# Gates in SBUF of their own between the marks of the next batch's front, and the back-transposes in the bank of the value products

## The reference

```python
q, k = x @ Wq, x @ Wk                                  # 16 heads of 64
w, sel = top_k(x @ Ws, 2)                              # per token and head, 2 of 8 experts
mix_v = sum_k sigmoid(w) * one_hot(sel)                # "gates"
v = einsum('bthe,bted->bhtd', mix_v, x @ Wv)           # "values"
probs = softmax(q * scale @ k^T)                       # 512 x 512 a head
attn = einsum('bhij,bhjd->bihd', probs, v)             # "heads"
mask_o = one_hot(top_k(x @ Wd, 2)).sum()               # also of "gates"
res = einsum('bthe,bthd,efd->bthf', mask_o, attn, Wo)  # "mixed" and "result"
```

## Time and profile before

| | |
|---|---|
| median of 3 runs | 3077.64 us (3067.38 to 3088.6) |
| the profiled execution, its own time | 3074.05 us |
| its span | 3072.2 us, 45343 instructions |
| PE busy | 2509.0 us (82%) |
| DVE busy | 1559.2 us (51%) |
| ACT busy | 1348.7 us (44%) |
| POOL busy | 808.0 us (26%) |
| mean granted TensorE clock | 0.919 |

### The profile page before, as it was taken

How to read it: one execution, slowest core, us unless ns; L and a number is a source line. 1 busy time by engine, 2 the same in 40 slices (tenths; PEclk the granted TensorE clock), 3 DMA queues, 4 the chain that set the end, 5 groups by cost and what they waited for, 6 DMA issues and landing times. The chain is left out here.

```text
span 3072.2 us, 45343 instructions
## 1 busy us (share of the span) xinstructions
PE 2509.0 (82%) x15660; PEld 1542.5 (50%) x15660; DVE 1559.2 (51%) x2646; ACT 1348.7 (44%) x2913; POOL 808.0 (26%) x370
## 2 busy tenths in 40 slices
PE   3984699779897898879897798978988798986476
PEld 2353346554475445654465544744456544653254
DVE  4235753546635384464735465353844557337622
ACT  0231226553464525554264534545255543653254
POOL 1003520106401092013701064011910136004500
PEclk7896799999898998999899998989999999999798
DMA  2110010112001030012101030011200121001001
GB/s 74 41 48 8 11 52 1 39 31 74 15 15 42 24 77 2 15 56 49 40 1 54 17 76 12 15 42 42 60 2 15 56 55 32 15 15 39 0 29 32
DMA packets 210737, 101.65 MB, mean 33 GB/s; under 512 B 137367, under 2 KB 189620, under 8 KB 210492
## 3 DMA queue, kind: packets, MB, share of 16 engines
q1 hardware_dynamic: 205052, 95.74, 11.3%
q10 hardware_dynamic: 5440, 2.75, 0.3%
HBM read 77.48 MB, written 20.99 MB: 32 GB/s over the span
## 5 line engine op out<-in xcount | busy, mean ns | idle before, releaser
L1508 DVE TENSOR_REDUCE nmax<-bank 128x1 f32<-128x512 f32 x512 | 340.9, 686 | 654.4 <-PE bank L971 652.5
L689 POOL TENSOR_TENSOR prod<-pv,mixv 128x1024 f32<-128x1024 f32 x184 | 608.5, 3343 | 239.9 <-ACT pv L1133 168.1
L1169 ACT ACTIVATE prT<-bank 128x512 f32<-128x512 f32 x512 | 305.5, 597 | 666.8 <-PE bank L704 662.3
L971 PE MATMUL bank<-keys,qs 64*128 64x512 f32 x1024 | 325.7, 714 | 245.2 <-DVE on L1502 99.8
L628 POOL TENSOR_TENSOR rstd<-vareps,minus_half 128x4 f32<-128x4 f32 x48 | 50.0, 1042 | 1474.9 <-DVE vareps L1276 1474.8
L1182 ACT ACTIVATE pr<-bank,nmax 128x512 f32<-128x512 f32 x512 | 349.4, 685 | 97.6 <-DVE nmax L1508 97.1
L704 PEld LDWEIGHTS bank<-ident,pr 128*128 128x128 f32 x2048 | 244.9, 152 | 267.1 <-issue 234.5
L704 PE MATMUL bank<-ident,pr 128*128 128x128 f32 x2048 | 357.8, 301 | 25.9 <-ACT prT L1169 25.8
L1075 ACT ACTIVATE arena<-bank 128x512 f32<-128x512 f32 x256 | 152.8, 597 | 467.0 <-PE bank L816 422.9
L1008 PE MATMUL bank<-prT,vals 128*64 128x128 f32 x4096 | 297.1, 290 | 59.1 <-ACT prT L1169 58.8
L1473 DVE TENSOR_REDUCE vals<-prod 128x128 f32<-128x1024 f32 x256 | 306.5, 1207 | 36.7 <-POOL prod L689 36.7
(11 more groups left out here) (220 smaller groups left out, 3064.7 us busy)
## 6 DMA issues: line engine op xcount, KB each, us to landing
Wg<-in_L_ffn_Wg SPq DMA_DIRECT2D x64, 256.0 KB, 2.8
Wu<-in_L_ffn_Wu SPq DMA_DIRECT2D x64, 256.0 KB, 3.1
Wd<-in_L_ffn_Wd SPq DMA_DIRECT2D x64, 256.0 KB, 3.8
out_rows<-on SPq DMA_DIRECT2D x32, 512.0 KB, 2.6
onR<-out_rows SPq DMA_DIRECT2D x32, 512.0 KB, 3.9
xin<-in_L_attn_x SPq DMA_DIRECT2D x8, 256.0 KB, 4.3
mask_rows<-masko SPq DMA_DIRECT2D x8, 256.0 KB, 4.2
maskR<-mask_rows SPq DMA_DIRECT2D x8, 256.0 KB, 6.9
```

Source lines behind the costliest of these rows:

```text
L689: g.tensor_tensor(*value_piece(n), ALU.mult).then_inc(vprod_r[0], 1)
L971: pe.matmul((S0, S1)[(turn + odd) % 2][:, :], qs[half, j % 3, r, :], keys[half, p, :], start=True, stop=True).then_inc(s_ps[0], 1)
L1169: s.activation(prT[:, m % 3, :], TB[:, :], ACT.Copy).then_inc(pT_r[0], 1)
L1508: v.tensor_reduce(nmax[:, m % 2:m % 2 + 1], (S0, S1)[turn % 2][:, :], X_AXIS, ALU.max, negate=True).then_inc(nmax_r[0], 1)
```

## The change

Two things are done. **Gates:** gate, eq, cand, oh1 and oh2 get SBUF tensors of their own, attn0's wait for mix_g goes, and a new function `fronts` puts attn1 first and then the 13 marks of the gates between the 28 marks of load, attn0 and moe_in. **Back:** the transposes go to OB, with a semaphore of their own (back_ps); a back takes no turn of S0 and S1 any more; the value products that come next in OB wait for on_r; the back steps move to heads 11 and 3, and in the finish two rest steps earlier.

```diff
-BACK_AT = (14, 6)
+BACK_AT = (11, 3)
-    steps += [("rest", 0)] * 5 + [("back", 2 * NT - 1)] + [("rest", 0)] * 4
+    steps += [("rest", 0)] * 3 + [("back", 2 * NT - 1)] + [("rest", 0)] * 6
-TURN = [sum(kind != "rest" for kind, _ in HEAD_STEPS[:k + 1]) for k in range(len(HEAD_STEPS))]
+TURN = [sum(kind not in ("rest", "back") for kind, _ in HEAD_STEPS[:k + 1]) for k in range(len(HEAD_STEPS))]
-        gate = part(0, [2, NT, HS, NE])
-        eq = part(1024, [2 * NT * HS, NE])
...
+        gate = sb("gate", [P, 2, NT, HS, NE])
+        eq = sb("eq", [P, 2 * NT * HS, NE])[:, :, :]
...
+        back_ps = sem("back_ps", 2 * NT)
...
+            def fronts(b, offset=0):
+
+                first = of(FRONT_A, b, offset + 1)
+                gates, others = [(*("gates", (b, offset)), [m]) for m in range(1, MARKS["gates"] + 1)], []
+                for name, at in first:
+                    others += [(name, at, [m]) for m in range(1, MARKS[name] + 1)]
+                both = [gates[0]]
+                for n, mark in enumerate(others):
+                    both.append(mark)
+                    if n % 2 == 0 and n // 2 + 1 < len(gates):
+                        both.append(gates[n // 2 + 1])
+                return of(("attn1",), b, offset) + both
...
-                schedule(stages, [(of(("heads",), b, -1), of(FRONT_B, b) + of(FRONT_A, b, 1))])
+                schedule(stages, [(of(("heads",), b, -1), fronts(b))])
...
+                wait(pe, on_r, b, 0)
                 for n in range(NQ * NT):
...
-                    elif what == "back":
-                        wait(pe, on_r, b, y + 1)
...
-                    elif kind != "rest":
+                    elif kind not in ("rest", "back"):
                         free(b, turn)
...
-                            last = pe.transpose(bank_k[:, p * P:(p + 1) * P], oaT[:, NJ * (x % 2) + p, :], ident[:, :])
-                        last.then_inc(s_ps[0], 1)
+                            last = pe.transpose(OB[:, p * P:(p + 1) * P], oaT[:, NJ * (x % 2) + p, :], ident[:, :])
+                        last.then_inc(back_ps[0], 1)
...
                             wait(pe, oa_r, b, m // GROUP)
+                            if h % (HS // 2) == 1:
+                                wait(pe, on_r, b, m // (HS // 2))
...
-                wait(v, mix_g, b, 0)
...
-                        wait(v, s_ps, b, turn)
-                        v.tensor_tensor(on[:, half, :], (S0, S1)[turn % 2][:, :].rearrange("p (h d) -> p h d", d=DS), rden[:, m % 2, :].unsqueeze(2).to_broadcast([P, HS // 2, DS]), ALU.mult).then_inc(on_r[0], 1)
+                        wait(v, back_ps, b, m + 1)
+                        v.tensor_tensor(on[:, half, :], OB[:, :].rearrange("p (h d) -> p h d", d=DS), rden[:, m % 2, :].unsqueeze(2).to_broadcast([P, HS // 2, DS]), ALU.mult).then_inc(on_r[0], 1)
```

More of the change, by code:

```diff
@@ L230, in build @@
         hdB = sb("hdB", [P, T])
-        gate = part(0, [2, NT, HS, NE])
-        eq = part(1024, [2 * NT * HS, NE])
-        cand = part(2048, [2 * NT * HS, NE])
-        oh1 = part(3072, [2 * NT * HS, NE])
-        oh2 = part(4096, [2 * NT * HS, NE])
+        gate = sb("gate", [P, 2, NT, HS, NE])
+        eq = sb("eq", [P, 2 * NT * HS, NE])[:, :, :]
+        cand = sb("cand", [P, 2 * NT * HS, NE])[:, :, :]
+        oh1 = sb("oh1", [P, 2 * NT * HS, NE])[:, :, :]
+        oh2 = sb("oh2", [P, 2 * NT * HS, NE])[:, :, :]
         top = sb("top", [P, 2, 2 * NT * HS])
@@ L1413, in gates @@
             def gates(b):
-                g = gate.rearrange("p g i h e -> p (g i h) e")
+                g = gate[:, :, :, :, :].rearrange("p g i h e -> p (g i h) e")
                 n = 2 * NT * HS
```

## The result

The changed kernel takes 3088.39 us (median of 20 runs, 3083.99 to 3095.44), the kernel before, measured beside it, 3076.56 us (20 runs, 3065.01 to 3088.60). The ratio is 1.0043, 95% interval 1.0031 to 1.0054: 0.4% slower, where 2.2% faster was forecast. The profiled execution spans 3086.2 us at a mean granted clock of 0.923; before it was 3072.2 us at 0.919.

The account below looks back on a forecast made before the run. PE, busy 82% of the span, was taken as the bound, its scores' wait for `on` as the longest touchable item. Terms gave 11.6 us a pass, 70 in six, less 3 outside: 3009 us as median, range 2955 to 3075.

Parts of the forecast that it names:

- (a): At PE's score matmul: scores no longer wait for `on`, 15.2 us less a pass.
- the wait only moves: Rival at the scores: late DVE delays nmax and exponentials, so the wait returns there; no gain, some 3075 us; chance 0.12.
- (h): Clock in three stretches of the first half granted 0.50: half of 7.4 us regained, 3.7 a pass.
- (e): At the gates' first mark: DVE still stands at top, PE first makes one pair of scores; 1.9 us lost a pass.
- (g): In the gates' stretch: attn0's projections partly cover other latency waits; 4.0 us gained a pass.
- (b): At the first half's backs of tiles 1 to 3: the next products wait uncovered for `on`; 3.7 us lost a pass.
- (d): At attn0's mark 2: DVE's 4.2 us burst, one step before a back, delays PE's products; 2.4 us lost a pass.
- (c): At the second half's backs: the back waits for ACT's copy of OB; 2.3 us lost a pass.
- (f): In POOL's queue: cand runs while DVE normalises and slows it; 1.0 us lost a pass.
- the rival's 8.6: Lock rival: POOL's five gate operations each hold DVE for their length, 8.6 us a pass, 3055 us; chance 0.06.
- interleaving does nothing: Rival at the gates: their chain stays serial, so latency cover and clock gain are lost; 3055 us; chance 0.15.
- The ring: Rival in OB: products, copy, back, `on` and next products follow each other uncovered in one bank; 3150 us; chance 0.08.

Follow-up runs that it names:

- e2: The kernel before with the gates' own SBUF, the new order `fronts`, no mix_g wait, the back left in S0 and S1; 3040.98 us, 0.9862.
- e8: e6 with the gates' marks moved so that DVE's burst at attn0's mark 2 comes after that back's `on`; 3068.96 us, 0.9957.
- e9: e8 with the GELU marks run two by two and no gates mark between attn0's marks 16 and 20; 3067.55 us, 0.9955.
- e5: The changed kernel with PE's back put behind the transposes of its step; 3070.21 us, 0.9986.
- e10: The kernel before with only the gates' own SBUF and without the mix_g wait, in the old order; 3068.90 us, 0.9974.
- e1: The changed kernel with the old order of the front (gates first, then the next batch's front); 3110.17 us, 1.0084.
- e11: The changed kernel without PE's back transposes; DVE's `on` reads the copy oaT and the products don't wait for it; 3028.12 us, 0.9854.
- e6: e5 with the first half's back of tiles 0 to 2 one head earlier, before head 10 and the mixed step; 3065.56 us, 0.9969.
- e12: e6 with the result step of a tile two heads later (RESULT_AT 14 for 12); 3081.38 us, 1.0022.

## Why the prediction was wrong

**Step (a) failed.** It credited all of the 15.2 us a pass that the scores waited for `on`. In the third pass 7.4 came back as waits for exponentials, above the 5 that the forecast had named as its sign of being wrong, and 3.5 as waits for xout at the same scores, so that 4.3 were gained; with e2 as the base, where the interleaving has already taken its part, the move of the back gave the scores 16.0 - 15.0 = 1.0 us a pass. The rows of the forecast held the reason: DVE's queue was late, and the maximum stands in that queue too. The text said so under "the wait only moves", and argued against it that three of the four causes had been moved from the backs. They had; but they then stood ahead of a maximum or an xout, as the timeline of the gates' first mark shows. That rival, with a chance of 0.12 and a price of 3075, was the nearest to 3088; what it lacked was xout, whose place among the front's marks had no term in the sum. With 4.3 for (a), nothing for (h) and (e) left out because its wait is already among the 7.4, the forecast's own sum is 4.3 - 9.4 + 4.0 = -1.1 a pass, which is the mean loss of the six passes; that it agrees so closely is partly luck, since 4.3 is read from one pass and (a) and (g) shorten the same waits. How much of the 7.4 is each pair's own chain and how much the shifted order stays open.

**(b) and (d)**, `on` exposed at the products: 3.7 + 2.4 = 6.1 us forecast, 5.5 measured, inside the 5 to 8 named beforehand. (b)'s three products waited 0.93, 0.93 and 2.36, together 4.2, and tile 0's, put at nothing, 0.29; (d)'s waited 1.04 where 2.4 was taken. As a wait the size was right; in e8 and e9 a quarter to a third less of it bought no time that can be measured.

**(c)**, the wait for ACT's copy: 2.3 forecast, 3.1 measured, at the four second halves' backs that it was put for (0.86, 0.61, 1.14, and 0.48 in the finish) and at none of the first halves'. It matters more than its length, as what stands behind it is held too: e5 won back 18 us (3088.39 to 3070.21) by the place of the back within its step alone.

**(e)**, the gates' first mark: 1.9 forecast, 1.88 measured, as a wait for the exponential, behind one pair of scores as foreseen, and `top` again with over 4 us of idle ahead of it.

**(f)**, POOL beside DVE: 1.0 a pass taken. DVE's 128 normalisations of h took 63.0 us before and 68.8 after, 5.8 more, 1.0 a pass; in e2 they took 74.0, 1.8 a pass more. DVE's busy time as a whole did not grow with the change (1559.2 and 1559.0). The four beside cand took 2.92 us, as the pair of the earlier trace rows said. So the slowing was seen, and the rival's 8.6 a pass was not; the rule of the Trainium skill (SBUF — State Buffer, Who interferes with whom) that the prediction tells agrees in kind, since a normalisation of four ran long beside one POOL operation, but not every POOL operation cost its length.

**(g)**, the front's work covering the gates' latencies: 4.0 a pass forecast. The order alone brought 0.989, 34 us, 5.7 a pass (e10 to e2), and on top of the moved back 12.6 us by the ratios or 21.8 by the medians, 2.1 to 3.6 a pass (e1 to the changed kernel). The rival "interleaving does nothing" was wrong, and it is the one part of the change that pays.

**(h)**, the clock: 3.7 forecast, none seen where it was put. The first half of the third pass had 0.94 before and 0.93 after; waits of 3.5 and 4.5 us remain in it, where none over 2.4 was to be left. Over all 20 runs the changed kernel's mean granted clock was 0.923, against 0.914 to 0.917 of the kernel before beside the experiments, so a little of it may have come elsewhere.

**A slip in the sum:** 3007 and the 3.6 us to the median make 3011, not 3009; nothing hangs on it.

**The ring** did not come as priced (3150), but in part: in batch 7, with nothing beside the heads, the heads are 5.5 us longer, where 1.9 was forecast. The kernels with the back in the scores' banks took 190.4 to 194.9 us there, and e11, with no back at all, 196.3, so that not all of the changed kernel's 199.7 is the ring's. And what is held behind the back weighs more than `on`: e5 lowered the waits for oaT and prT by 12.6 and 11.3 us while that for `on` rose by 8.8, and the kernel got faster.

**Open:** e6, the best of the versions with the back in OB, is still 1.1% behind e2. All of PE's waits sum to 547.5 us against e2's 527.0, and PE is busy 6.7 us longer, together 27.2 for a difference in span of 26.2; the six kinds above make 277.6 against 257.1, and the rest of the waits cancel. But whether another order of marks would free xout and the maximum was not tried beyond e8, e9 and e12.

## What to carry to other kernels

Here a wait that the trace puts down to one releaser was worth only what lay between that releaser and the next one at the same instruction: add all waits at that instruction, and ask which other input comes from the same late queue, before crediting the whole. Taking a step out of a hand-written order also shifts every later pairing of steps with the work beside them, so look up what each step then stands behind. And a change of two parts is to be run in its parts: here one gained 1.4% and the other lost more than that.

## What the runs showed of the hardware

A table load on ACT took 1.283 us and nothing beyond it: the load at 1377.70 begins 0.02 us after the copy before it ends, and the exponential 0.01 us after the load. The Trainium skill (ScalarE: Activation LUTs, What ACT_TABLE_LOAD costs) gives the same 1283 ns and a drain of about 1380 ns on top; no such gap stands in these rows. From 67 loads to 43 the time of the kernel did not change measurably (0.9862 and 0.9879), with ACT busy 45% and 44% of the span; since the pairing brought PE 19.1 us of waits for GELUs, this does not show that the loads cost nothing.
